# A decoder layer on one core: the statistics of the first norm in sums of four, their roots read from PSUM by ScalarE, and a set of constants made later

## The chip, the core and the metric

The kernel runs on one core of one Trainium2 chip. Its engines are called PE (TensorE's matmuls, with PEld for its weight loads), DVE (VectorE), ACT (ScalarE), POOL (GpSimd) and SP (SyncE, which here issues DMAs). Each has its own list of instructions and waits for others on semaphores. The metric is device time of one execution in microseconds (us), lower is better. Three runs of the kernel before gave a median of 2107.65 us (2106.93 to 2108.5). About 0.2% of it, 4.2 us, can be told from no change.

## The reference

All in float32, with x of 2 batches x 512 tokens x 1024. The change lies in the first lines: the layer norm and the first projection of the Mamba block.

```python
x = x + attn(_layernorm(x))          # Mamba-2 block and a gated MLP
x = x + xattn(_layernorm(x), ctx)    # quantised matmul with the context
x = x + ffn(_layernorm(x))           # three matmuls with binarised differences

def _layernorm(x, axis=-1, eps=1e-05):
    m = jnp.mean(x, axis=axis, keepdims=True)
    v = jnp.var(x, axis=axis, keepdims=True)
    return (x - m) / jnp.sqrt(v + eps)

# attn begins:
h = hidden * rsqrt(mean(hidden * hidden) + EPS) * ln1_w
zxbcdt = h @ w_in.T                                   # w_in: 2568 x 1024
z, xs, Bs, Cs, dt = split(zxbcdt, [1024, 1280, 1536, 2560])
xBC = silu(causal_conv4(concat(xs, Bs, Cs)) + conv_b) # 12 tiles of 128 columns
dt = softplus(dt + dt_bias)                           # 8 columns, one for each head
# ... chunked state space scan with dt, cumulative sums of dt * A, gate by silu(z), @ w_out
```

## The kernel before

The tokens lie in the free dimension, the 1024 features on 128 partitions x 8 blocks (k = 0 to 7). A batch is one half of 512 columns. For exact float32 products each operand is split in a rounded high part and the rest, and a product is three matmuls (hi x hi, lo x hi, hi x lo); ACT writes the high part (`weights_hi`, `act_hi`), DVE subtracts it for the low one (`weights_lo` L1737, `act_lo` L2095).

The **head** (to about 57 us) takes one batch after the other. DVE adds the blocks in pairs (`head_pair` L2084), PE sums the four pairs over the partitions by matmuls with a matrix of 1/1024 (`head_mean` L866), DVE takes the mean from each block (`head_centre` L2089), ACT makes `act_hi` (L1532) and the squares (L1520), DVE `act_lo`. PE multiplies each block, as it becomes ready, with the first two blocks of weights (`first_half` L882, six matmuls for a block and a batch). DVE adds the squares in pairs (L2101), PE sums them (`head_var` L873), DVE scales the sum (L2105), ACT takes logarithm and exponential of it (`head_root` L1525, L1526, behind a table load L1523), and DVE mends the root by a Newton step (`head_rsqrt` L2110 to L2112). The tables of constants (`constants` L1747 to L1771, 23 small instructions of DVE) stand between the two batches. The products of the normed input with the 8 columns for dt (L913, L915, 32 matmuls) follow when both batches are through.

The **conv stage** (57 to 176 us) has six pairs of weight blocks. A block is 48 matmuls (L849) on PE. DVE multiplies what comes out by the root (L2162), makes the low part of the weights two blocks on (L1737), and runs the four taps of the convolution (L2168, three of L2170); ACT applies silu and makes `weights_hi`. PE starts a block when its weights are ready (`raw_consumed`) and DVE has taken the product that was in the same bank (`conv_product_taken`). After the third pair DVE clears `minus_cs_wide` (L2221) and scales six blocks of the input (L2187). In the middle of the fifth pair DVE writes the cumulative sums into `minus_cs_wide` (L2231), which PE transposes (L936) before the sixth pair.

Every engine works through its list in the order that is written, so an instruction that waits holds up all that stands behind it on its engine.

## Time and profile before

| | |
|---|---|
| Median of three runs | 2107.65 us |
| Profiled execution, its own time | 2109.02 us |
| Its span, first to last instruction | 2106.9 us |
| PE busy | 2081.3 us (99%) |
| DVE busy | 1679.2 us (80%) |
| ACT busy | 1055.6 us (50%) |
| Mean granted TensorE clock | 0.998 |

### The profile page before, as it was taken

The numbers are of one execution on the slowest core, as the hardware profiler recorded it, in microseconds if no ns is written. First come the engines' busy times: TensorE is split into PE (matmuls) and PEld (weight loads), VectorE is DVE, ScalarE is ACT, GpSimd is POOL, SyncE is SP. The second block draws the span as 40 slices with busy tenths as digits, with TensorE's granted clock in tenths as the row PEclk, the third lists the DMA queues.
The fourth block names the chain that finished last, engine by engine and source line by source line (L and its number), as shares of the span: only waits on it lengthen the run. The fifth ranks groups of instructions, "written<-read, shape, count | busy, mean of one in ns | idle before, by whom it ended". The sixth has DMA issues, their size and how long they took to land.

```text
span 2106.9 us, 26518 instructions
## 1 busy us (share of the span) xinstructions
PE 2081.3 (99%) x9230; PEld 1670.4 (79%) x9234; DVE 1679.2 (80%) x2526; ACT 1055.6 (50%) x1748; POOL 186.1 (9%) x296
## 2 busy tenths in 40 slices
PE   8999999999999999999999999999999999999999
PEld 4777778788888888888888855888888888888887
DVE  8888686797777888888879898977677776698886
ACT  5333244457777777774444366533333333444442
POOL 0001101101111112110000002010000000100000
PEclk9999999999999999999999999999999999999999
DMA  3151116539889999897430045554444443846101
GB/s 137 38 206 54 51 61 196 149 112 324 289 298 332 326 348 351 294 343 263 141 140 1 1 180 116 170 195 147 171 146 175 161 150 123 321 176 208 52 21 60
DMA packets 136434, 370.07 MB, mean 176 GB/s; under 512 B 16688, under 2 KB 27568, under 8 KB 132656
## 3 DMA queue, kind: packets, MB, share of 16 engines
q1 hardware_dynamic: 110640, 287.12, 39.1%
q0 software_dynamic: 25088, 80.23, 11.1%
q8 instruction: 74, 1.21, 0.2%
q10 hardware_dynamic: 576, 1.05, 0.1%
q14 instruction: 56, 0.46, 0.1%
HBM read 288.12 MB, written 84.41 MB: 177 GB/s over the span
## 4 chain that ended last, share of the span: by engine, by line
PE 88%; DVE 9%; ACT 2%; issue 1%; DMA 0%; ACTq 0%; DVEq 0%
PE pair L1086 47%; PE pair L1134 24%; PE pair L856 7%; PE pair L1030 2%; DVE conv_out L2170 2%; PE pair L849 1%; PE pair L1096 1%; PE pair L1167 1%; DVE weights_lo L1737 1%; PE pair L968 1%; PE pair L989 1%; PE pair L1161 1%; PE pair L995 0%; DVE comb_lo L1905 0%; DVE hs L2089 0%
## 5 line engine op out<-in xcount | busy, mean ns | idle before, releaser
L1086 PE MATMUL pair<-comb_hi,ring_hi 128*128 128x512 f32 x1456 | 566.7, 389 | 0.0
L1086 PE MATMUL pair<-comb_hi,ring_lo 128*128 128x512 f32 x1456 | 566.5, 389 | 0.0
L1086 PE MATMUL pair<-comb_lo,ring_hi 128*128 128x512 f32 x1456 | 566.5, 389 | 0.0
L1134 PE MATMUL pair<-inner_ring_a,ring_hi 128*128 128x512 f32 x1080 | 332.8, 389 | 0.0
L1086 PEld LDWEIGHTS pair<-comb_hi,ring_hi 128*128 128x128 f32 x1456 | 273.3, 188 | 58.1 <-issue 1.4
L1086 PEld LDWEIGHTS pair<-comb_lo,ring_hi 128*128 128x128 f32 x1456 | 273.3, 188 | 56.8
L1086 PEld LDWEIGHTS pair<-comb_hi,ring_lo 128*128 128x128 f32 x1456 | 273.3, 188 | 56.6
L1134 PEld LDWEIGHTS pair<-inner_ring_a,ring_hi 128*128 128x128 f32 x1080 | 202.6, 188 | 42.1
L1134 PE MATMUL pair<-inner_ring_a,ring_lo 128*128 128x512 f32 x540 | 210.1, 389 | 0.0
L1360 ACT ACTIVATE ring_hi<-ring_sum 128x512 fp32r<-128x512 f32 x160 | 100.5, 631 | 147.4 <-DVE ring_sum L1818 145.4
L1833 DVE TENSOR_TENSOR ring_lo<-raw_a,ring_hi 128x512 fp32r<-128x512 f32 x146 | 99.7, 688 | 54.6 <-ACT ring_hi L1360 52.8
L1134 PE MATMUL pair<-inner_ring_b,ring_hi 128*128 128x512 f32 x432 | 133.5, 390 | 0.0
L1134 PEld LDWEIGHTS pair<-inner_ring_a,ring_lo 128*128 128x128 f32 x540 | 101.3, 188 | 21.1
L1833 DVE TENSOR_TENSOR ring_lo<-ring_sum,ring_hi 128x512 fp32r<-128x512 f32 x160 | 109.9, 687 | 10.0 <-ACT ring_hi L1360 7.8
L856 PE MATMUL pair<-act_hi,weights_hi 128*128 128x512 f32 x256 | 108.5, 424 | 1.7 <-DVE act_lo L2272 1.4
L1984 DVE TENSOR_TENSOR pair<-coeff_in 128x1024 f32<-128x1024 f32 x84 | 103.1, 1227 | 0.0
L856 PE MATMUL pair<-act_hi,weights_lo 128*128 128x512 f32 x256 | 100.0, 390 | 0.0
L856 PE MATMUL pair<-act_lo,weights_hi 128*128 128x512 f32 x256 | 99.8, 390 | 0.0
L1486 ACT ACTIVATE sign_out<-pair 128x1024 int8<-128x1024 f32 x84 | 85.3, 1016 | 24.3 <-DVE pair L1984 24.3
L1134 PEld LDWEIGHTS pair<-inner_ring_b,ring_hi 128*128 128x128 f32 x432 | 81.1, 188 | 17.3 <-issue 0.5
L1360 ACT ACTIVATE ring_hi<-raw_a 128x512 fp32r<-128x512 f32 x146 | 87.4, 624 | 10.6 <-DVE raw_a L1813 7.0
L1360 ACT ACTIVATE ring_hi<-comb_hi_f 128x512 fp32r<-128x512 f32 x72 | 45.4, 630 | 94.0 <-PE pair L1134 47.9
(395 smaller groups left out, 3616.1 us busy)
## 6 DMA issues: line engine op xcount, KB each, us to landing
coeff_in<-f_gu SPq DMA_DIRECT2D x56, 512.0 KB, 5.2
coeff_in<-b_gu SPq DMA_DIRECT2D x56, 512.0 KB, 7.0
weights_raw<-w_mamba SPq DMA_DIRECT2D x44, 512.0 KB, 3.5
raw_a<-w_gu SPq DMA_DIRECT2D x28, 512.0 KB, 6.2
raw_a<-w_gu SPq DMA_DIRECT2D x56, 256.0 KB, 6.0
u_spill<-gate_a POOLq DMA_DIRECT2D x56, 256.0 KB, 5.2
coeff_in<-f_dn SPq DMA_DIRECT2D x28, 512.0 KB, 4.5
coeff_in<-b_dn SPq DMA_DIRECT2D x28, 512.0 KB, 6.7
```

Of the source, the lines that this page charges most:

```text
L849: ins = pe.matmul(out[:, HALF[half]], w[:, wi, k * P:(k + 1) * P], a(half, k), start=k == 0 and n == 0, stop=k == KT - 1 and n == 2)
L856: ins = pe.matmul(out, w[:, wi, k * P:(k + 1) * P], a(b, k), start=k == 0 and n == 0, stop=k == KT - 1 and n == 2, skip_group_check=True)
L968: pe.matmul(ps[2][:, g * 512:(g + 1) * 512], bx_cur[:, 2 + g, :], xbc[:, 4 + g * HPG:4 + (g + 1) * HPG, b * SEQ + c * P:b * SEQ + (c + 1) ...
L989: ins = pe.matmul(ps[2][:, hd * P:(hd + 1) * P], x_dt[:, hd, :], att[:, hd, :], start=True, stop=c == 0)
L1030: ins = pe.matmul(out, wt[:, slot, col], a, start=j % 2 == 0 and kk == 0 and n == 0, stop=j % 2 == 1 and kk == KH - 1 and n == 2, skip_gro ...
L1086: ins = pe.matmul(out, wt[:, slot, col], a, start=t in (0, 1, 3) and kk == 0 and n == 0, stop=kk == KH - 1 and n == 2, skip_group_check=True)
L1134: ins = pe.matmul(out, wt[:, slot, col], a, start=t in (0, 1, 3) and k == 0 and n == 0, stop=k == SC_PAIRS - 1 and n == 2, skip_group_chec ...
L1360: act.activation(WRH[:, slot, :], src, ACT.Copy).then_inc(s_whi, 1)
L1486: act.activation(sign_out[:, c % 2, :], dif_ps[:, :], ACT.Sign).then_inc(s_sign, 1)
L1833: TT(WRL[:, slot, :], src, WRH[:, slot, :].bitcast(F32), ALU.subtract).then_inc(s_wlo, 1)
L1984: TT(dif_ps[:, :], dif[:, c % 2, 0, :], dif[:, c % 2, 1, :], ALU.subtract).then_inc(s_cd, 1)
L2170: ins = STT(tile[:, :, back:], src[:, :, :SEQ - back], conv_par[:, s, TAPS - 1 - back:TAPS - back], tile[:, :, back:], ALU.mult, ALU.add)
```

## The change

In the head, for the second batch the four pair sums are added to two by DVE (`head_four`) before PE sums them, and so are the squares of the first batch; the squares of the second batch stay four pair sums. The eight products for dt of the first batch stand on PE before the second batch's blocks (`dt_half`), those of the second behind its variance. The first batch's variance stands on PE behind block 4 of the second, and two of the four variance products of the second batch behind its block 6. ACT reads the variance sums from PSUM, with scale and bias in the instruction, for the logarithm and for a copy that DVE's Newton step uses; DVE's scaling goes. ACT's wait for the first root moves from behind block 4 to behind block 6, and one of two table loads goes. The constants, but for the two instructions on `w_dt`, move behind the third pair of the conv stage. The low part of the fourth weight block (`weights_lo(4, 1, 1)`) moves from ahead of the second root to behind the first product of the conv stage. Waits that count semaphores are renumbered to suit.

```diff
         for k in range(KT):
             first_half(k, 0)
-            if k >= KT // 2:
-                head_mean(1, k - KT // 2)
-        head_var(0)
+            if k == KT - 2:
+                head_mean(1, 0, 0, 7, False)
+        head_mean(1, 1, 2, 10, True)
+        pe.wait_ge(s_const, 3)
+        dt_half(0)
         for k in range(KT):
             first_half(k, 1)
-        head_var(1)
+            if k == 4:
+                head_var(0, 0, 4, 15, False)
+                head_var(0, 1, 8, 16, True)
+            if k == 6:
+                head_var(1, 0, 4, 17, False)
+                head_var(1, 1, 6, 18, False)
+        head_var(1, 2, 8, 19, False)
+        head_var(1, 3, 10, 20, True)
+        dt_half(1)
...
         def head_root(b):
-            act.preload_act_table_set("natural_log_exp_and_others")
-            act.wait_ge(s_ht, b + 1)
-            own.then(act.activation(scr_u(4)[:, HALF[b]], scr_u(6)[:, HALF[b]], ACT.Ln))
+            act.wait_ge(s_hvar, HEAD_VARS[b])
+            own.then(act.activation(scr_u(4)[:, HALF[b]], ps[3][:, HALF[b]], ACT.Ln, bias=EPS * EPS, scale=(1.0 + EPS) / DM))
             act.activation(root_in[:, HALF[b]], scr_u(4)[:, HALF[b]], ACT.Exp, scale=-0.5).then_inc(s_hroot, 1)
+            act.activation(scr_u(6)[:, HALF[b]], ps[3][:, HALF[b]], ACT.Identity, bias=EPS * EPS, scale=(1.0 + EPS) / DM).then_inc(s_ht, 1)
...
-                if b == 1 and k == 4:
+                if b == 1 and k == 2:
+                    act.preload_act_table_set("natural_log_exp_and_others")
+                if b == 1 and k == 6:
                     head_root(0)
...
+        def head_four(b, first, second, sums):
+            dve.wait_ge(s_hpair, sums)
+            TT(xbc[:, first, HALF[b]], xbc[:, first, HALF[b]], xbc[:, second, HALF[b]], ALU.add).then_inc(s_hpair, 1)
...
+            if k == 3:
+                dt_weights()
             if k >= KT // 2:
                 head_pair(1, k - KT // 2)
-        for j in range(KT // 2):
-            head_square_pair(0, j)
-        constants()
+            if k == KT // 2 + 1:
+                head_four(1, 0, 1, 6)
+        head_four(1, 2, 3, 9)
+        head_square_pair(0, 0)
+        head_square_pair(0, 1)
         head_centre(1, 0)
         head_centre(1, 1)
+        head_square_pair(0, 2)
         for k in range(KT):
             if k + 2 < KT:
                 head_centre(1, k + 2)
             head_lo(1, k)
-            if k == 1:
-                head_var(0)
-            if k >= 3 and k % 2 == 1:
-                head_square_pair(1, (k - 3) // 2)
-        head_square_pair(1, KT // 2 - 1)
+            if k == 0:
+                head_square_pair(0, 3)
+            elif k == 1:
+                head_four(0, 4, 6, 12)
+            elif k == 2:
+                head_four(0, 8, 10, 14)
+            elif k < 5:
+                head_square_pair(1, k - 3)
+            elif k > 5:
+                head_square_pair(1, k - 4)
         head_rsqrt(0)
         weights_lo(3, 0, 0)
-        weights_lo(4, 1, 1)
-        head_var(1)
         head_rsqrt(1)
...
             TT(conv_in, ps[s][:, :], root_in, ALU.mult).then_inc(s_taken, 1)
+            if n == 0 and s == 0 and lo is None:
+                weights_lo(4, 1, 1)
...
         conv_pair(2)
+        constants()
         dve.memset(cs_wide[:, :, :], 0.0)
         scale_hs(range(2, KT))
         conv_pair(3)
```

The order of ACT in the second batch of the head, the stretch that holds the first root. Before:

```order
L1532 ACTIVATE act_hi<-hs,params 128x512 [waits norm_centred]
L1520 ACTIVATE conv_out<-hs 128x512
L1523 ACT_TABLE_LOAD
L1525 ACTIVATE scratch_r<-scratch_r 128x512 [waits norm_var_ready]
L1526 ACTIVATE scratch_r<-scratch_r 128x512 [waits act_steps]
L1532 ACTIVATE act_hi<-hs,params 128x512 [waits norm_centred]
L1520 ACTIVATE conv_out<-hs 128x512
L1532 ACTIVATE act_hi<-hs,params 128x512 [waits norm_centred]
L1520 ACTIVATE conv_out<-hs 128x512
L1532 ACTIVATE act_hi<-hs,params 128x512 [waits norm_centred]
L1520 ACTIVATE conv_out<-hs 128x512 x3
```

And the same engine now, from `act_hi` of block 5 on (`pair` is PSUM, `conv_out` in the head holds the squares):

```order
L1543 ACTIVATE act_hi<-hs,params 128x512 [waits norm_centred]
L1531 ACTIVATE conv_out<-hs 128x512
L1543 ACTIVATE act_hi<-hs,params 128x512 [waits norm_centred]
L1531 ACTIVATE conv_out<-hs 128x512
L1535 ACTIVATE scratch_r<-pair 128x512 [waits norm_var_summed]
L1536 ACTIVATE scratch_r<-scratch_r 128x512 [waits act_steps]
L1537 ACTIVATE scratch_r<-pair 128x512
L1543 ACTIVATE act_hi<-hs,params 128x512 [waits norm_centred]
L1531 ACTIVATE conv_out<-hs 128x512 x3
```

The root has moved from between blocks 4 and 5 to between blocks 6 and 7; it waits on PE's sums themselves, and one `act_hi` and three squares stand behind it.

The order of DVE from the second root to the first taps of the conv stage. Before, from the first root's last step:

```order
L2112 SCALAR_TENSOR_TENSOR scratch_r<-scratch_r 128x512 [waits dve_steps]
L1737 TENSOR_TENSOR weights_lo<-weights_raw,weights_hi 128x1024 [waits weights_hi_ready,dve_steps]
L1737 TENSOR_TENSOR weights_lo<-weights_raw,weights_hi 128x1024 [waits weights_hi_ready]
L2105 TENSOR_SCALAR scratch_r<-pair 128x512 [waits norm_var_summed]
L2110 SCALAR_TENSOR_TENSOR scratch_r<-scratch_r 128x512 [waits norm_root_ready]
L2111 TENSOR_TENSOR scratch_r<-scratch_r 128x512 [waits dve_steps]
L2112 SCALAR_TENSOR_TENSOR scratch_r<-scratch_r 128x512 [waits dve_steps]
L2178 COPY conv_par<-params 128x10 [waits conv_summed,dve_steps]
L2162 TENSOR_TENSOR scratch_r<-pair,scratch_r 128x1024 [waits conv_summed,block_used,dve_steps]
L2168 TENSOR_SCALAR conv_out<-scratch_r,conv_par 128x1024 [waits conv_product_taken]
```

And now:

```order
L2127 SCALAR_TENSOR_TENSOR scratch_r<-scratch_r 128x512 [waits dve_steps]
L1750 TENSOR_TENSOR weights_lo<-weights_raw,weights_hi 128x1024 [waits weights_hi_ready,dve_steps]
L2124 SCALAR_TENSOR_TENSOR scratch_r<-scratch_r 128x512 [waits norm_root_ready]
L2126 TENSOR_TENSOR scratch_r<-scratch_r 128x512 [waits norm_var_ready,dve_steps]
L2127 SCALAR_TENSOR_TENSOR scratch_r<-scratch_r 128x512 [waits dve_steps]
L2203 COPY conv_par<-params 128x10 [waits conv_summed,dve_steps]
L2185 TENSOR_TENSOR scratch_r<-pair,scratch_r 128x1024 [waits conv_summed,block_used,dve_steps]
L1750 TENSOR_TENSOR weights_lo<-weights_raw,weights_hi 128x1024 [waits weights_hi_ready]
L2193 TENSOR_SCALAR conv_out<-scratch_r,conv_par 128x1024 [waits conv_product_taken]
```

One `weights_lo` has moved from ahead of the second root's wait to between the first product and its taps.

The order of DVE between the third and the fourth pair of the conv stage. Before:

```order
L2170 SCALAR_TENSOR_TENSOR conv_out<-scratch_r,conv_par,conv_out 128x2x509 [waits dve_steps]
L2221 MEMSET minus_cs_wide 128x576
L2187 TENSOR_TENSOR hs<-hs,scratch_r 128x1024 x6
L2178 COPY conv_par<-params 128x10 [waits conv_summed]
L2162 TENSOR_TENSOR scratch_r<-pair,scratch_r 128x1024 [waits conv_summed,block_used,dve_steps]
L1737 TENSOR_TENSOR weights_lo<-weights_raw,weights_hi 128x1024 [waits weights_hi_ready]
```

And now, the last four of the constants and what follows them:

```order
L1783 TENSOR_REDUCE row_scale<-tri_ident_mask 128x1 [waits dve_steps]
L1784 TENSOR_REDUCE row_scale<-tri_ident_mask 128x1 [waits dve_steps]
L1785 TENSOR_TENSOR row_scale<-row_scale 128x1 [waits dve_steps]
L2247 MEMSET minus_cs_wide 128x576 [waits dve_steps]
L2212 TENSOR_TENSOR hs<-hs,scratch_r 128x1024 x6
L2203 COPY conv_par<-params 128x10 [waits conv_summed]
L2185 TENSOR_TENSOR scratch_r<-pair,scratch_r 128x1024 [waits conv_summed,block_used,dve_steps]
L1750 TENSOR_TENSOR weights_lo<-weights_raw,weights_hi 128x1024 [waits weights_hi_ready]
```

The constants (21 rows in all) stand ahead of the clearing, the six scalings and the low weights of the ninth block.

## Rows read from the trace of the kernel before

**Rows 1.** Chain of waits, 110 to 160 us (start us, us, what).
```profile
125.28 1.13 DVE weights_lo L1737
...
150.39 0.40 DVE minus_cs_wide L2231 x3
...
150.83 2.71 PE pair L936 x16
```

**Rows 2.** Waits of PE, 60 to 200 us (total us, times, longest).
```profile
PE pair L936 <- DVE minus_cs_wide L2231: 2.3, 1, 2.3
...
PE pair L849 <- DVE weights_lo L1737: 0.8, 1, 0.8
```

**Rows 3.** Busy time by windows (stretch, us, engines with counts, PEclk, DMA).
```profile
126.40:130.00 3.60, 3.53 (x15) 2.92 (x16) 3.49 (x5) 0.00 (x0) 0.00 (x0) 1.00 1.04 400
148.50:150.80 2.30, 0.03 (x1) 0.00 (x0) 2.23 (x9) 0.74 (x1) 0.00 (x0) 1.00 0.22 75
150.80:155.40 4.60, 4.57 (x21) 4.15 (x22) 1.85 (x2) 2.66 (x3) 0.00 (x0) 0.63 0.45 162
```

**Rows 4.** Timeline of PE, head (start us, us, engine, line, what).
```profile
30.31 1.02 PE L866 MATMUL pair<-conv_out,ones_over_dm 128*128 128x512 f32 x2
31.16 3.60 PE L873 MATMUL pair<-conv_out,ones 128*128 128x512 f32 x8
...
44.12 0.39 PE L882 MATMUL pair<-act_hi,weights_hi 128*128 128x512 f32 x1
...
45.48 0.39 PE L882 MATMUL pair<-act_hi,weights_hi 128*128 128x512 f32 x1
...
49.88 0.79 PE L913 MATMUL pair<-act_hi,w_dt_hi_lo 128*16 128x512 f32 x1
...
57.68 0.62 PE L849 MATMUL pair<-act_hi,weights_hi 128*128 128x512 f32 x2
```

**Rows 5.** Timeline of DVE, 17 to 81 us.
```profile
17.75 0.75 DVE L2095 SCALAR_TENSOR_TENSOR act_lo<-hs,params,act_hi 128x512 fp32r<-128x512 f32 x1
18.42 0.68 DVE L2089 TENSOR_TENSOR hs<-hs,pair 128x512 f32<-128x512 f32 x1
...
28.34 0.22 DVE L1747 CAST ident_bf<-tri_ident_mask 128x128 bf16<-128x128 f32 x1
...
28.61 0.19 DVE L1749 CAST w_dt_hi_lo<-w_dt 128x64 fp32r<-128x64 f32 x1
...
29.11 0.16 DVE L1752 TENSOR_TENSOR minus_head_pick<-tri_ident_mask 128x8 f32<-128x8 f32 x1
...
31.79 0.16 DVE L1771 TENSOR_TENSOR row_scale<-row_scale 128x1 f32<-128x1 f32 x1
32.28 1.88 DVE L2089 TENSOR_TENSOR hs<-hs,pair 128x512 f32<-128x512 f32 x3 [0.33 <-DVE row_scale L1771]
...
52.75 0.69 DVE L2110 SCALAR_TENSOR_TENSOR scratch_r<-scratch_r 128x512 f32<-128x512 f32 x1 [1.36 <-ACT scratch_r L1526]
...
55.14 1.23 DVE L2162 TENSOR_TENSOR scratch_r<-pair,scratch_r 128x1024 f32<-128x1024 f32 x1
56.40 0.81 DVE L2168 TENSOR_SCALAR conv_out<-scratch_r,conv_par 128x1024 f32<-128x1024 f32 x1
...
78.14 1.23 DVE L2162 TENSOR_TENSOR scratch_r<-pair,scratch_r 128x1024 f32<-128x1024 f32 x1
...
80.42 0.81 DVE L2168 TENSOR_SCALAR conv_out<-scratch_r,conv_par 128x1024 f32<-128x1024 f32 x1
```

**Rows 6.** Timeline of ACT, second batch of the head.
```profile
39.87 0.63 ACT L1525 ACTIVATE scratch_r<-scratch_r 128x512 f32<-128x512 f32 x1
40.54 0.63 ACT L1526 ACTIVATE scratch_r<-scratch_r 128x512 f32<-128x512 f32 x1
41.07 0.71 ACT L1532 ACTIVATE act_hi<-hs,params 128x512 fp32r<-128x512 f32 x1
41.69 0.62 ACT L1520 ACTIVATE conv_out<-hs 128x512 f32<-128x512 f32 x1
```

More of the change, by code:

```diff
@@ L32 @@
 ORDER = (1, 0)
+HEAD_SUMS = 20
+HEAD_VARS = (2, 6)
 Y_AT = {5: (0, 1, 2), 6: (3, 4, 5), 7: (6, 7)}
@@ L861, in _, with head_mean, head_var, dt_half @@
         pe.sem_inc(s_stage, 1)
-        def head_mean(b, j):
-            pe.wait_ge(s_hpair, b * (KT // 2) + j + 1)
-            ins = pe.matmul(ps[2][:, HALF[b]], ones_mean[:, :], xbc[:, j, HALF[b]], start=j == 0, stop=j == KT // 2 - 1)
-            if j == KT // 2 - 1:
+        def head_mean(b, n, tile, sums, last):
+            pe.wait_ge(s_hpair, sums)
+            ins = pe.matmul(ps[2][:, HALF[b]], ones_mean[:, :], xbc[:, tile, HALF[b]], start=n == 0, stop=last)
+            if last:
                 ins.then_inc(s_hm, 1)
-        def head_var(b):
-            for j in range(KT // 2):
-                pe.wait_ge(s_hpair, KT + b * (KT // 2) + j + 1)
-                pe.matmul(ps[3][:, HALF[b]], ones[:, :], xbc[:, 4 + 2 * j, HALF[b]],
-                          start=j == 0, stop=j == KT // 2 - 1).then_inc(s_hvar, 1)
+        def head_var(b, n, tile, sums, last):
+            pe.wait_ge(s_hpair, sums)
+            pe.matmul(ps[3][:, HALF[b]], ones[:, :], xbc[:, tile, HALF[b]], start=n == 0, stop=last).then_inc(s_hvar, 1)
+        def dt_half(b):
+            for k in range(KT):
+                pe.matmul(ps[2][0:2 * HEADS, HALF[b]], wdt_hl[:, k, :, :], ah(b, k),
+                          start=k == 0, stop=False, skip_group_check=True)
+                ins = pe.matmul(ps[2][0:HEADS, HALF[b]], wdt_hl[:, k, 0, :], al(b, k),
+                                start=False, stop=k == KT - 1, skip_group_check=True)
+            if b == 1:
+                ins.then_inc(s_dtm, 1)
         def first_half(k, b):
@@ L906, in conv_pair @@
                 conv_block(i, s)
-        pe.wait_ge(s_const, 4)
-        for b, half in enumerate(HALF):
-            for k in range(KT):
-                pe.matmul(ps[2][0:2 * HEADS, half], wdt_hl[:, k, :, :], ah(b, k),
-                          start=k == 0, stop=False, skip_group_check=True)
-                ins = pe.matmul(ps[2][0:HEADS, half], wdt_hl[:, k, 0, :], al(b, k),
-                                start=False, stop=k == KT - 1, skip_group_check=True)
-        ins.then_inc(s_dtm, 1)
         conv_pair(1)
@@ L1198, in _ @@
         feed_forward(W_END[0] - 4, W_END[0] - 2)
-        ctx_var(bank(1), x_square_a, range(KH), 2 * KT, (), 0)
+        ctx_var(bank(1), x_square_a, range(KH), HEAD_SUMS, (), 0)
         feed_forward(W_END[0] - 2, W_END[0])
@@ L1218, in _ @@
         column_sums(1, bank(3))
-        ctx_var(bank(7), x_square, range(KH), 2 * KT + KH, (), 0)
+        ctx_var(bank(7), x_square, range(KH), HEAD_SUMS + KH, (), 0)
         pe.wait_ge(s_mc, 2)
@@ L1246, in _ @@
         pe.wait_ge(s_xt, 6)
-        ctx_var(bank(7), x_square, range(KH), 2 * KT + 2 * KH, (), 0)
+        ctx_var(bank(7), x_square, range(KH), HEAD_SUMS + 2 * KH, (), 0)
         pe.wait_ge(s_rlo, 2)
@@ L1265, in _ @@
         pe.wait_ge(s_ht, 4 + BATCH + 2)
-        ctx_var(bank(7), x_square, range(3), 2 * KT + 3 * KH, (6, 7), 5 * KT)
+        ctx_var(bank(7), x_square, range(3), HEAD_SUMS + 3 * KH, (6, 7), 5 * KT)
         second_mean(0, bank(6))
@@ L1744, in _, with dt_weights @@
         dve.sem_inc(s_yt, 1)
+        def dt_weights():
+            own.then(dve.tensor_copy(wdt_hl[:, :, 0, :], wdt[:, :, :]))
+            TT(wdt_hl[:, :, 1, :], wdt[:, :, :], wdt_hl[:, :, 0, :].bitcast(F32), ALU.subtract).then_inc(s_const, 1)
         def constants():
-            dve.wait_ge(s_par, 48)
             dve.tensor_copy(ident_bf[:, :], ident).then_inc(s_const, 1)
             dve.tensor_copy(mask_bf[:, :], mask).then_inc(s_const, 1)
-            own.then(dve.tensor_copy(wdt_hl[:, :, 0, :], wdt[:, :, :]))
-            own.then(TT(wdt_hl[:, :, 1, :], wdt[:, :, :], wdt_hl[:, :, 0, :].bitcast(F32), ALU.subtract))
             dve.memset(coef3[:, :], 0.0)
@@ L2124, in _ @@
                 head_centre(0, k + 3)
+            if k == 3:
+                dt_weights()
             if k >= KT // 2:
                 head_pair(1, k - KT // 2)
-        for j in range(KT // 2):
-            head_square_pair(0, j)
-        constants()
+            if k == KT // 2 + 1:
[3 more added lines that the diff above has]
+        head_square_pair(0, 1)
         head_centre(1, 0)
         head_centre(1, 1)
+        head_square_pair(0, 2)
         for k in range(KT):
```

8 lines of the change are left out of this document (3 added, 5 removed).

## Prediction

> **What bounds the kernel now.** I read the chain of waits first, then the waits of PE, then timelines of PE, DVE and ACT over the first 160 us, since all that is changed lies there. PE is busy nearly throughout, so it seems to be the bound. The chain says otherwise for the start: up to 150.8 us it runs over DVE, with the low weights of the ninth block and the writing of `minus_cs_wide`, and only from L936 on over PE [rows 1]. PE's waits agree: 0.8 us for those low weights and 2.3 us at L936 for DVE [rows 2]. So until L936 PE has 3.1 us to spare, and an edit there is worth what it does to DVE's arrival at `minus_cs_wide` (150.39). What follows is PE's own work and what PE releases, and it shifts with L936.
>
> One more thing hangs on that wait. In the wait PE is at the full clock in the records, and in 150.8 to 155.4 the mean granted clock is 0.63: most of it was at 1.2 GHz. Behind the 0.8 us wait it stays at 1.00 (2.4 GHz) [rows 3]. The low stretch took PE (1 - 0.63) x 4.6 = 1.7 us, on the chain.
>
> **The change, part by part.** I follow the changed lists in the durations of the rows: a DVE sum or centring steps by 0.60 (1.88 for three, the first ones overlapped), `act_lo` by 0.67 and is done after 0.75 [rows 5]; a float32 product with `ones` steps by 0.85 (30.31 to 31.16) and is done after 1.02, with handover 1.1; six matmuls of a block by 1.36 (44.12 to 45.48) [rows 4]; on ACT logarithm 0.67, exponential 0.53 (done 0.63), `act_hi` 0.62, square done after 0.62 [rows 6].
>
> *Start of the second batch.* Before, the fourth mean product starts at 30.31 with three such products in front of it among the blocks [rows 4]; now one stands in front of the last. Two less are 1.7 us. Against that DVE has the two instructions on `w_dt` (28.61 to 29.11, 0.5) and a sum of 0.6 to 0.7 ahead of the last `act_lo`, for which I allow PE a wait of 0.4. So the last product starts at 29.0, and the first centring at 30.1 to 30.2, where it was 32.28 behind the constants [rows 5]: 2.1 us won.
>
> *DVE's work there.* It gains four sums (two for the means, two for the squares) and the first batch's last two pair sums, and loses a scaling. Two centrings, a pair sum and a third centring (2.4) bring `act_lo` of block 0 to 32.6; each further block is centring, a sum and `act_lo`, 1.87. Block 4 starts at 32.6 + 4 x 1.87 = 40.1 and is done at 40.8. The eight dt products of the first batch take 16 of the 32 matmuls between 49.88 and 57.68 [rows 4], 3.9 us; from 29.9 to 33.7 they lie beside this and cost at most 0.3 at its start.
>
> *The new wait.* ACT now waits behind block 6 for the first variance, and PE makes it behind block 4: 40.8 + 1.36 = 42.2, two products, 0.85 + 1.1, so 44.2. ACT has stood there since about 41.4. Queued behind its wait are `act_hi` of block 7 and the squares of 5 to 7. Logarithm, exponential and the copy (0.67 + 0.53 + 0.53) end at 45.9, `act_hi` 0.62, square of block 5 done at 47.2. DVE stands too, as its next sum needs that square and `act_lo` of block 7 is behind the sum: 0.60 + 0.75, 48.6. PE, which had block 7 at 45.48 [rows 4], has it at 48.6. Then 1.36, two variance products (0.85 + 1.1) to 52.0, logarithm and exponential (0.67 + 0.63 and handover) to 53.4. There DVE's Newton step starts, 52.75 before [rows 5]. The 2.1 us are gone and 0.7 more.
>
> ACT reading PSUM with scale and bias is not in these rows; the nearest are a square at 0.62 and `act_hi`, which has a scale, at 0.71 [rows 6]. So it is between nothing and 0.1 more for each of four instructions; I take the logarithm's own 0.63, being the same function. The copy for the second root is hidden by the Newton step's first instruction (0.69). The table load that goes lay in a wait of ACT for DVE, so it gives nothing.
>
> *`weights_lo(4, 1, 1)`.* It stood in front of DVE's wait for the second root (1.36 idle [rows 5]), part of it free. Now it stands between the first product of the conv stage and its taps: with such an instruction there the step is 78.14 to 80.42, 2.28, without it 55.14 to 56.40, 1.26 [rows 5]. That is 1.0 more.
>
> *The constants.* What moves is 28.34 to 28.61 and 29.11 to 31.95, 3.1 us, and there were 0.33 us idle behind it [rows 5]: 3.1 to 3.45, I take 3.3. Behind the third pair DVE has no idle time to lay it in, and behind it are queued the clearing, six scalings, the next product and the low weights of block nine, for which PE already waited. POOL's store of the scaled input starts later by as much, and SP's loads, which wait for `raw_consumed`, move along; before, none of them held PE.
>
> DVE's arrival at `minus_cs_wide`: 0.7 + 1.0 + 3.3 = 5.0 us later. It hides what PE saves: four float32 products (3.4 us) fewer and the dt products earlier. PE would end the head about 2 us earlier (51.8 + 3.9 = 55.7 against 57.68), but the next block waits for the first product to be taken, 55.8 + 1.23 = 57.1.
>
> *The clock.* PE gets to block nine half a microsecond to one later than before and its weights come 5.0 later, so it waits 4 to 5 us there. That is longer than the wait at L936, behind which the clock fell, so I expect it to fall here, with up to 1.7 us lost in block nine. PE had 2.3 us to spare at L936, so this costs nothing in the end; it leaves 0.6 us of wait at L936, and behind a wait of 0.8 the clock did not fall [rows 2, 3]. The low stretch behind L936 then goes: 1.7 us back.
>
> Sum: + 5.0 - 1.7 = + 3.3 us. The profiled execution (2109.02, of it 2106.9 span) would be 2112.3; it lay 1.4 us above the median of the runs, 2107.65, which gives 2111.0.
>
> [...]
>
> **The rivals.**
> *Low clock twice (slower).* If the remaining wait at L936 is still followed by the low clock, nothing comes back, and the end is 5.0 us later: 2112.7. It decides if that wait stays near 2.3 us, as it does where the clock's fall lies mostly inside the long wait itself and costs block nine little. For it: the fall behind L936 came at once, within its 2.7 us [rows 1, 3]. Against it: block nine starts the work again right behind the wait, where a low stretch costs most.
> *PE is the bound after all (faster).* If the constants and the moved low weights find room on DVE, the four products less count: 2107.65 - 3.4 = 2104.2. Against it are both waits of PE for DVE.
> *ACT's wait does not bite.* If the first variance comes by the time ACT asks for it, about 3 us of the head come back; with 1.0 and 3.3 paid and the clock's 1.7 returned, DVE is 2.0 later and the end 0.3 later: 2108.0. Against it: the variance products stand behind block 4, whose `act_lo` DVE cannot give before 40.
>
> **How the numbers follow.** I give the forecast 0.66, the low clock twice 0.19, ACT's wait not biting 0.09, PE as the bound 0.06. The forecast's own range is 2109.6 to 2112.4: 0.35 either way for the constants, 0.4 for ACT's instructions, 0.5 for the head's handovers, and half a microsecond between runs. With the rivals, 8 in 10 lie in 2108.2 to 2113.2. The bound of 0.2% is 4.2 us: slower means over 2111.9, faster under 2103.4. Of the forecast a fifth lies above (0.13), of the first rival most (0.16): slower 0.29. Faster has the tail of PE as the bound, 0.04. The rest, 0.67, is the same within 0.2%.
>
> **What would show it.** Right: in the head ACT idle for about 3 us behind a square, waiting for L874, and DVE idle about 4 us in the middle of the second batch; the first product of the conv stage near 55.8; the constants as some 3 us of DVE ahead of the six scalings; PE waiting 4 to 5 us for the low weights of block nine with the low clock behind it, and less than 1.5 us at L936 with the full clock behind. Wrong: PE waiting at neither place, or DVE idle just ahead of the moved constants. A wait at L936 of over 2 us with the low clock behind it would be the first rival.

## The result and the profile after

The changed kernel takes 2114.44 us (median of 13 runs, 2111.3 to 2115.31), the kernel before 2107.65 (13 runs beside them, 2105.66 to 2111.2): the ratio is 1.0029, 95% interval 1.0022 to 1.0036, so 4.6 to 7.6 us slower; the medians lie 6.8 apart. The forecast was 2111.0, with a range of its own of 2109.6 to 2112.4 and one with the rivals to 2113.2, and it gave slower than 2111.9 a chance of 0.29: the direction was right, the size about half, and the time lies above both ranges. The profiled execution took 2115.17 us, its span is 2113.2.

The chain of waits of the changed kernel answers to [rows 1] (start us, us, what); the constants now stand in it, ahead of the scalings, and so do the low weights of block nine.

```profile
117.54 1.28 DVE conv_out L2195
118.82 0.14 DVE ident_bf L1763
...
121.71 0.16 DVE row_scale L1785
122.05 0.54 DVE minus_cs_wide L2247
122.59 6.75 DVE hs L2212 x6
129.46 1.23 DVE scratch_r L2185
130.68 1.13 DVE weights_lo L1750
...
155.78 0.40 DVE minus_cs_wide L2257 x3
156.22 1.97 PE pair L947 x16
```

`minus_cs_wide` is copied at 155.78, 5.39 us later than before, and L947 (L936 before) starts as much later. PE's waits from 60 to 200 us answer to [rows 2] (total us, times, longest):

```profile
PE pair L851 <- DVE weights_lo L1750: 3.1, 2, 1.9
PE pair L1000 <- DVE attention L2326: 0.8, 1, 0.8
PE pair L947 <- DVE minus_cs_wide L2257: 0.6, 1, 0.6
```

The wait for the low weights has grown from 0.8 to two waits of 3.1 together, and the wait at L947 has shrunk from 2.3 to 0.6. The windows answer to [rows 3] (stretch, us, busy of PE, PEld, DVE, ACT and POOL, PEclk, DMA):

```profile
81.00:90.00 9.00, 7.76 (x25) 6.14 (x26) 8.05 (x8) 2.00 (x2) 0.00 (x0) 0.62 0.18 58
130.00:132.00 2.00, 0.14 (x1) 0.14 (x2) 2.00 (x3) 0.00 (x0) 1.22 (x2) 1.00 0.37 147
132.00:140.00 8.00, 8.00 (x29) 6.37 (x29) 5.66 (x6) 3.29 (x3) 0.00 (x0) 0.79 1.01 369
155.00:157.20 2.20, 1.55 (x12) 1.13 (x11) 2.17 (x8) 1.73 (x2) 0.00 (x0) 1.00 0.32 102
157.20:162.00 4.80, 4.80 (x28) 4.09 (x26) 1.97 (x3) 1.67 (x2) 0.00 (x0) 1.00 0.35 134
```

Behind L947 the clock stays full, as forecast; PE is at 1.2 GHz for part of block nine (0.79), as forecast, and also at 82 us (0.62), which was not. The head, on PE, ACT and DVE, answers to [rows 4 to 6]:

```profile
29.87 1.02 PE L868 MATMUL pair<-conv_out,ones_over_dm 128*128 128x512 f32 x2
...
41.58 0.50 PE L891 MATMUL pair<-act_hi,weights_hi 128*128 128x512 f32 x1 [0.20 <-DVE act_lo L2109]
...
43.08 1.88 PE L874 MATMUL pair<-conv_out,ones 128*128 128x512 f32 x4
...
49.31 0.50 PE L891 MATMUL pair<-act_hi,weights_hi 128*128 128x512 f32 x1
...
50.81 1.88 PE L874 MATMUL pair<-conv_out,ones 128*128 128x512 f32 x4
```

```profile
44.99 0.60 ACT L1535 ACTIVATE scratch_r<-pair 128x512 f32<-128x512 f32 x1 [2.85 <-PE pair L874]
45.62 0.63 ACT L1536 ACTIVATE scratch_r<-scratch_r 128x512 f32<-128x512 f32 x1
46.16 0.58 ACT L1537 ACTIVATE scratch_r<-pair 128x512 f32<-128x512 f32 x1
```

```profile
30.93 1.28 DVE L2103 TENSOR_TENSOR hs<-hs,pair 128x512 f32<-128x512 f32 x2 [1.24 <-PE pair L868]
...
47.90 0.69 DVE L2119 TENSOR_TENSOR conv_out<-conv_out 128x512 f32<-128x512 f32 x1 [3.86 <-ACT conv_out L1531]
...
54.02 0.69 DVE L2124 SCALAR_TENSOR_TENSOR scratch_r<-scratch_r 128x512 f32<-128x512 f32 x1 [0.85 <-ACT scratch_r L1536]
...
56.41 1.22 DVE L2185 TENSOR_TENSOR scratch_r<-pair,scratch_r 128x1024 f32<-128x1024 f32 x1
57.55 1.21 DVE L1750 TENSOR_TENSOR weights_lo<-weights_raw,weights_hi 128x1024 fp32r<-128x1024 f32 x1
58.68 0.81 DVE L2193 TENSOR_SCALAR conv_out<-scratch_r,conv_par 128x1024 f32<-128x1024 f32 x1
```

ACT waits 2.85 us and DVE 3.86, as forecast (3 and 4); the first product of the conv stage is at 56.41, 1.27 later than before (0.7 forecast).

### The profile page after: what moved, and what is told of

It is laid out like the page before. It is cut to its first block, busy times and chain, and to the rows that moved or that the text cites. A ratio compares the mean times of both kernels' runs of the same rounds, so it can differ in the third digit from the quotient of the medians.

```text
span 2113.2 us, 26506 instructions
## 1 busy us (share of the span) xinstructions
PE 2084.5 (99%) x9222; PEld 1672.7 (79%) x9226; DVE 1680.1 (80%) x2528; ACT 1055.6 (50%) x1749; POOL 184.8 (9%) x296
## 3 DMA queue, kind: packets, MB, share of 16 engines
q8 instruction: 74, 1.21, 0.2%
## 4 chain that ended last, share of the span: by engine, by line
PE 89%; DVE 7%; ACT 2%; issue 1%; DMA 1%; SPq 0%; ACTq 0%; DVEq 0%
PE pair L1097 47%; PE pair L1145 24%; PE pair L858 7%; PE pair L1041 2%; DVE conv_out L2195 2%; PE pair L851 1%; PE pair L891 1%; PE pair L1107 1%; PE pair L1178 1%; PE pair L979 1%; PE pair L1000 1%; DVE weights_lo L1750 1%; DMA sign_in_cd<-sign_spill 1%; PE pair L1172 1%; PE pair L1006 0%
```

## The experiments

Of every profile the table gives the first product of the conv stage, the step from it to the copy of `minus_cs_wide`, the copy, PE's wait for it, the time from L936's successor to the writing of `b_token_major`, all in us, and under "runs" the median less that of the kernel before, run beside it (where only a profile was taken, the one run's time).

| kernel | first product | step | copy | wait | to b | runs |
|---|---|---|---|---|---|---|
| before | 55.14 | 95.25 | 150.39 | 2.3 | 34.96 | |
| e6 before again | 55.40 | 95.23 | 150.63 | 2.3 | 33.36 | -0.7 |
| e11 before, third | 56.24 | 95.25 | 151.49 | 2.3 | 33.37 | 0.0 |
| e12 before, fourth | 55.57 | 95.25 | 150.82 | 2.3 | 33.35 | +0.1 |
| changed | 56.41 | 99.37 | 155.78 | 0.6 | 33.36 | +6.8 |
| e1 changed again | 56.27 | 99.41 | 155.68 | 0.7 | 33.32 | +5.5 |
| e16 changed, third | 57.32 | 99.42 | 156.74 | 2.3 | 34.97 | +8.1 |
| e2 constants in a wait | 57.09 | 97.01 | 154.10 | 1.5 | 33.33 | +4.0 |
| e3 low weights back | 56.29 | 98.41 | 154.70 | none | 33.29 | +3.1 |
| e4 before, constants moved | 55.96 | 98.41 | 154.37 | 0.7 | 33.36 | +3.2 |
| e7 constants back | 59.09 | 96.25 | 155.34 | 2.3 | 33.36 | +3.9 |
| e8 root behind block 7 | 56.46 | 99.44 | 155.90 | 2.3 | 34.98 | +4.7 |
| e9 variance back | 53.06 | 99.42 | 152.48 | none | 33.30 | +1.5 |
| e10 dt late | 56.62 | 99.42 | 156.04 | under 0.2 | 33.35 | +5.6 |
| e5 back in parts | 52.51 | 95.31 | 147.82 | 2.3 | 33.34 | -4.3 |
| e13 before, filled | 55.16 | 95.21 | 150.37 | 2.3 | 33.37 | +0.8 |
| e14 changed, filled | 55.77 | 99.41 | 155.18 | 0.7 | 33.36 | +4.5 |
| e15 parts, filled | 52.75 | 95.30 | 148.05 | 2.3 | 33.34 | -3.5 |

**The two terms behind the head.** e1 is the changed kernel unaltered.

> The changed kernel as it is, for a second profile of it. The chain theory (DVE's arrival at minus_cs_wide sets the time, and what PE does behind the conv stage only shifts) expects L947 again 5.0 to 5.5 us later than before, the end of the conv stage 3.5 to 4 us later, and the rest of the kernel the same length as before to within 0.5 us; then the whole is about 4 us slower. The tail theory (the 2.5 us that the first profile shows between 1220 and 1330 us belong to the change) expects those 2.5 us there again, and 6 us in all. If they are chance, the 1220 to 1330 stretch is as long as before in this profile or differs by another amount.

2113.86 us against 2108.38, ratio 1.0027 (1.0015 to 1.0038), so 3.2 to 8.0 us slower, about 4 expected; the step to the copy repeats to 0.04 us. The low stretches that the first profile showed in the tail at 1235.9 and 1293.9 us are missing (e16 has the first of them), and the span is 2109.7: their 2.5 us come and go with the run. e2 puts the constants into DVE's wait for the second norm's root:

```
             TS(scr(3), ps[3][:, :], scale, bias, ALU.mult, ALU.add).then_inc(s_ht, 1)
+            if between is not None:
+                between()
             dve.wait_ge(s_hroot, BATCH + n)
...
-        rsqrt(1, lambda j: scr_u(j + 1), 1.0 / DM, EPS)
+        rsqrt(1, lambda j: scr_u(j + 1), 1.0 / DM, EPS, constants)
...
         conv_pair(2)
-        constants()
```

> The changed kernel with the constants moved into DVE's wait for the root of the second norm (2.33 us idle in the profile of the changed kernel at 71.8 us). The chain theory expects 3.3 us less behind the third pair and about 0.9 us more at the root, so minus_cs_wide about 2.3 us earlier than in the changed kernel, and a time 2 to 2.5 us below it. The clock theory (PE's new short waits and the low clock behind them make the loss, not DVE's work) expects PE's wait for the low weights of block nine gone with the low clock behind it, but the end of the conv stage no more than 0.5 us earlier, and the time with it.

2112.39, ratio 1.0017 (1.0008 to 1.0026). The step falls by 2.4, about the 2.33 us that DVE waited there (up to 74.15 in the changed kernel's timeline); the rest of the 3.3 sticks out. The first product lies 0.8 later than in e1, so the copy comes 1.6 sooner; the time is 1.5 under e1's, where 2 to 2.5 were expected, and the two intervals overlap. PE does not wait for the low weights of block nine any more. e3 undoes the other term:

```
+        weights_lo(4, 1, 1)
         head_rsqrt(1)
...
-            if n == 0 and s == 0 and lo is None:
-                weights_lo(4, 1, 1)
```

> The changed kernel with the low part of the fourth weight block made ahead of the second root again, as before. DVE waited 0.85 us for that root in the changed kernel, so the chain theory expects the first product of the conv stage 0.3 us later, its taps 0.85 us earlier, and everything up to minus_cs_wide 0.85 us earlier; the time 0.5 to 1 us below the changed kernel. If the move cost nothing, as a wait behind it would take it up, minus_cs_wide stays where it is to 0.2 us.

2111.45, ratio 1.0019 (1.001 to 1.0028): the step falls by 1.0, and so does the copy. The time is 2.4 under e1's, more than the 0.5 to 1 expected; the intervals overlap here too. e4 is the kernel before with the constants alone moved behind the third pair (the two instructions on `w_dt` stay where they were):

```
-        constants()
+        dt_weights()
         head_centre(1, 0)
...
         conv_pair(2)
+        constants()
```

> The kernel before with the constants alone moved behind the third pair of blocks (the two instructions on w_dt stay between the batches). The chain theory expects the second batch's first centring 0.8 us earlier (PE's last mean product then sets it), the constants to cost 3.3 us later, minus_cs_wide 2.5 us later than before, PE waiting about 4 us for the low weights of block nine, and the time 0.8 us (if the low clock behind L936 goes) to 2.5 us above before. If PE were the bound, the time would be 0.6 us below before.

2111.54, ratio 1.0014 (1.0005 to 1.0023). The step is 3.16 longer than before. The head gives back less than the 0.8 expected: the first product comes at 55.96, against 56.24 in e11, the profile of before with the same low stretch of the clock at 14 us, so 0.3 sooner. Between the batches of the kernel before, the constants lay mostly in time in which DVE would have waited for PE's last mean product (33.10 in e4, with 3.44 us of waiting for it); the change took them out of a nearly free place. e7 puts them back in the changed kernel:

```
         head_square_pair(0, 1)
+        constants()
         head_centre(1, 0)
...
         conv_pair(2)
-        constants()
```

> The changed kernel with the constants between the two batches again, where they stood before; all else as changed. The chain theory: VectorE reaches the second batch 3 us later, but PE's eight dt products of the first batch stand ahead of its blocks and cover 2 of it or more; behind the third pair 3.1 to 3.3 us come back. The first product of the conv stage at 57.4 to 59.5, the step from it to the copy of minus_cs_wide 96.1 to 96.3 us (99.3 in the changed kernel, 95.25 before), the time 0 to 2.2 us under the changed kernel's. If the cost of the constants lay not in their place but in the clock, the step would stay over 98.

2112.35, ratio 1.0018 (1.0009 to 1.0027). The step is 96.25, the 1.0 of the low weights over before, but the head is 2.8 later: between the batches of the changed kernel, where PE's means come sooner, the constants cost nearly what they cost behind the third pair. Only in a wait are they free.

**The head.** e8 lets ACT do `act_hi` of block 7 and the squares ahead of the first root:

```
-                if b == 1 and k == 6:
-                    head_root(0)
...
             head_square(b, KT - 1)
+        head_root(0)
         weights_hi(2, 0)
```

> The changed kernel with ScalarE's first root behind the act_hi of block 7 and the squares, instead of behind block 6: what was queued behind the wait (act_hi of block 7, three squares) goes first. My forecast held that this wait costs the head some 3 us. If so, PE has block 7 some 2 us sooner than 49.3 us, the first product of the conv stage moves from 56.3 to about 53.5 to 54.5, and the time falls by 2 to 3 us. The rival: PE is what the head hangs on, since the eight dt products (3.9 us) stand ahead of its blocks and each block follows the one before without a gap; then the variance comes when PE gives it, the first product moves by less than 0.6 us, and the time by as little.

2113.16, ratio 1.0022 (1.0011 to 1.0033). The root runs without a wait and the 3.86 us in which DVE stood ahead of the last `act_lo` are gone, yet PE has block 7 at 49.07 instead of 49.31 (timelines of e8: ACT, then PE, then DVE):

```profile
45.18 0.60 ACT L1535 ACTIVATE scratch_r<-pair 128x512 f32<-128x512 f32 x1
```

```profile
47.76 1.88 PE L874 MATMUL pair<-conv_out,ones 128*128 128x512 f32 x4
49.07 0.80 PE L891 MATMUL pair<-act_hi,weights_hi 128*128 128x512 f32 x1
```

```profile
56.46 1.23 DVE L2184 TENSOR_TENSOR scratch_r<-pair,scratch_r 128x1024 f32<-128x1024 f32 x1
```

Block 4 starts 0.19 later in e8 (41.77), so the longest waits of the head in the changed kernel cost block 7 some 0.4 us and the first product 0.1: in e8 PE works without a gap from block 4 on, and its order alone sets the end. e10 takes the dt products out of that order ahead of the blocks:

```
-        dt_half(0)
         for k in range(KT):
             first_half(k, 1)
...
+        dt_half(0)
         dt_half(1)
```

> The changed kernel with the first batch's eight dt products (16 matmuls, 3.7 us of PE) at the end of the head beside the second's. If they cost what the order on PE suggests, the first block of the second batch starts up to 3.7 us sooner and the first product of the conv stage too. If VectorE's 1.87 us per block paces PE up to block 4 (PE waits 0.2 us for act_lo at each of blocks 2, 3 and 4 in the changed kernel), they are hidden: the first product stays within 0.4 us of 56.3 and the time within 1 us of the changed kernel's.

2113.11, ratio 1.0027 (1.0017 to 1.0037): hidden, first product at 56.62. In their place PE waits for the first `act_lo` of the batch, and the clock falls behind that wait; block 4 starts at 41.80 (41.58 in the changed kernel).

```profile
34.35 0.52 PE L891 MATMUL pair<-act_hi,weights_hi 128*128 128x512 f32 x1 [3.24 <-DVE act_lo L2109]
```

e9 takes back the variance by fours with its order on DVE, ACT and PE, puts the dt products late as e10 does, and leaves the rest (of the edit, the lines of PE's variance):

```
+        for j in range(KT // 2):
+            head_var(0, j, 4 + 2 * j, 11 + j, j == KT // 2 - 1)
         for k in range(KT):
             first_half(k, 1)
-            if k == 4:
-                head_var(0, 0, 4, 15, False)
-                head_var(0, 1, 8, 16, True)
-            if k == 6:
-                head_var(1, 0, 4, 17, False)
-                head_var(1, 1, 6, 18, False)
-        head_var(1, 2, 8, 19, False)
-        head_var(1, 3, 10, 20, True)
+        for j in range(KT // 2):
+            head_var(1, j, 4 + 2 * j, 15 + j, j == KT // 2 - 1)
```

> The changed kernel with the variance sums and products as before (by pairs, behind all blocks of a batch), the first root behind block 4 and the dt products at the end of the head; the second batch's mean by fours, the constants behind the third pair and the late low weights of the fourth block stay as changed. If VectorE's arrival is a plain sum of terms, the first product of the conv stage comes at 52.5 us (56.3 in the changed kernel), the step from it to minus_cs_wide stays 99.4, the copy comes at 151.9 and the time is 1 to 1.5 us over that of the kernel before, 4 to 4.5 under the changed kernel's. If the terms overlap (VectorE gives back what it won, because PE paces it between 56 and 148 us), the copy stays over 153.5 and the time 3 us or more over before.

2108.98, ratio 1.0009 (1.0 to 1.0018). The first product comes at 53.06, 3.2 to 3.4 sooner than in the first two profiles of the changed kernel, and the step stays 99.42: the terms add. The wait (e8) and the dt products (e10) being without effect, each taken away by itself, what cost the head is the variance by fours. PE's timelines share the 3.35 us in two: block 4 starts at 41.58 instead of 40.21, 1.4 later, and from there to the products for dt behind the last variance product PE takes 10.55 us instead of 8.57, 2.0 more. The first part is DVE's pace: it gives a block every 1.86 us up to block 4, where in e9 it gives the first four every 1.26 with no sum between them (`act_lo` of the first blocks, DVE, changed kernel and e9):

```profile
33.33 0.75 DVE L2109 SCALAR_TENSOR_TENSOR act_lo<-hs,params,act_hi 128x512 fp32r<-128x512 f32 x1
...
35.19 0.74 DVE L2109 SCALAR_TENSOR_TENSOR act_lo<-hs,params,act_hi 128x512 fp32r<-128x512 f32 x1
```

```profile
33.32 0.74 DVE L2105 SCALAR_TENSOR_TENSOR act_lo<-hs,params,act_hi 128x512 fp32r<-128x512 f32 x1
...
34.58 0.75 DVE L2105 SCALAR_TENSOR_TENSOR act_lo<-hs,params,act_hi 128x512 fp32r<-128x512 f32 x1
```

e5 is e9 with the low weights ahead of the second root and the constants split over two of DVE's waits, the second norm's root and the softplus exponential:

> Kept of the change: the second batch's mean from two sums of four, ScalarE reading the variance from PSUM, no constants between the batches. Back as before: the variance products by pairs behind all blocks of a batch, with the first root asked for behind block 4 of the second batch; the dt products at the end of the head; the low weights of the fourth block ahead of the second root. New: the constants lie in two of VectorE's waits, most of them while the second norm's root is made, the last few while the softplus exponential is made. The chain theory (everything before L936 is worth what it does to VectorE's arrival at minus_cs_wide): no instruction of VectorE is added ahead of the first product of the conv stage, the constants (3.1 us) leave its path, two float32 products leave PE's; the first product of the conv stage at 52.5 to 54 us (55.14 before), the copy of minus_cs_wide 1 to 2.6 us sooner than 150.39, and the time 1 to 3.4 us under that of the kernel before. PE then waits less or not at all at L936's successor. The rival (PE is the bound of the head whatever VectorE does, and the excess lies in low-clock stretches of the first 90 us): the time within 1 us of the kernel before.

2104.21 us against 2108.5, ratio 0.9982 (0.9973 to 0.9991): faster than both kernels, 3.8 us under before by the ratio. The step is that of before, 95.31, with all constants hidden, and the head is 3 us shorter. PE's wait at L936's successor is 2.3 as before, where less or none was expected, so DVE still sets the end there.

**The clock.** Three more profiles of before and one of the changed kernel:

> The kernel before, for a second profile. It tells whether the excess of the measured difference (5.5 to 6.8 us) over the 3.7 us seen at the end of the conv stage lies in the clock. If the extra low-clock stretches of the changed kernel (6.8 us instead of 3.4 at 14 us, one at 82 us, one at block nine) belong to its waits, the profile of before shows one of 3.4 us at 14 to 16 us, none at 82 and 133, one behind L936, again. If they come by chance of the run, this profile shows some of them as well, and minus_cs_wide then lies later than 150.39.

> The kernel before, a third profile, for the clock behind L936: PE waits 2.3 us there in both profiles so far, with 3.4 us at the low clock behind it in the one and none in the other. If the low stretch is a matter of chance, it is there in some of the profiles; L936 to the writing of b_token_major then takes 35.0 us with it and 33.4 without.

> The kernel before, a fourth profile, for the same question: 35.0 us from L936 to b_token_major with a low stretch behind the wait, 33.4 without one.

> The changed kernel, a third profile. In the first two the low clock of the head lasts 6.8 us; in before 3.4 in three profiles of four. If it is chance, this one may show 3.4 and the first product of the conv stage at 55.5 instead of 56.3; if it hangs on the change, 6.8 again. In the tail the first profile had low stretches at 1236 and 1294 us and the second none; L1207's successor to the second block there takes 59.2 or 57.5 us accordingly.

PE waits 2.3 us at L936 in all four of before, and in three no low clock follows; their runs took 2107.8, 2107.52 and 2107.56 us, against 2109.02 of the one with it. The windows behind it in e6 and e11, against 0.63 in [rows 3], and in e16, where the changed kernel has the wait of 2.3 and the low clock:

```profile
150.80:155.40 4.60, 4.33 (x27) 3.88 (x28) 1.69 (x5) 2.91 (x3) 0.00 (x0) 1.00 0.51 183
```

```profile
151.90:156.50 4.60, 4.57 (x28) 4.07 (x29) 1.11 (x1) 2.52 (x3) 0.00 (x0) 1.00 0.49 174
```

```profile
PE pair L947 <- DVE minus_cs_wide L2257: 2.3, 1, 2.3
```

```profile
157.20:161.80 4.60, 4.60 (x22) 4.12 (x23) 2.52 (x3) 2.61 (x3) 0.00 (x0) 0.64 0.45 167
```

Over all profiles here with a wait of 2.3 at that place the low clock follows in 3 of 10. At block nine the longer wait is not the surer one. In the first two profiles of the changed kernel and in e14 PE waits 1.9 to 2.0 us there, the clock falls behind it, and 0.6 to 0.7 are left at L947 with the full clock behind: the forecast's picture. In e16 and e8 PE waits 3.4 us at block nine, the clock stays at 1.00 (126 to 148 us), 2.3 are left at L947 and the low clock follows there: the sign that the forecast gave for its first rival. PE's waits for the low weights in e16:

```profile
PE pair L851 <- DVE weights_lo L1750: 4.6, 2, 3.4
```

In the head the low clock follows PE's wait of 3.8 us at 11 to 15 us in each of the fifteen profiles so far, but longer in the changed kernel (10 to 22 us of e6, then of the changed kernel):

```profile
10.00:22.00 12.00, 8.05 (x25) 5.03 (x24) 10.57 (x16) 9.53 (x15) 0.00 (x0) 0.86 0.82 310
```

```profile
10.00:22.00 12.00, 8.23 (x22) 5.55 (x21) 10.15 (x17) 9.16 (x14) 0.00 (x0) 0.72 0.83 315
```

It is 0.72 in all three of the changed kernel, and of before in e11 alone, whose first product is 0.67 to 1.1 us later than in the other three. e13, e14 and e15 fill that wait with four products whose result is not used, in before, in the changed kernel and in e5:

```
+        for _ in range(4):
+            pe.matmul(ps[3][:, HALF[0]], ones[:, :], xbc[:, 3, HALF[0]], start=True, stop=True)
```

> The kernel before with four float32 products more on PE, results unused, in its wait of 3.8 us for the first act_lo of the head (11 to 15 us); nothing else differs. The low clock at 14 to 17 us follows that wait: with the wait filled it should not come, whether it is 3.4 or 6.8 us long without. The first product of the conv stage then lies about 0.8 us ahead of 55.4 (a stretch longer by 3.4 us put it 0.85 later in one profile of before), at 54.3 to 54.8, minus_cs_wide at 149.5 to 150.1, and the time falls by 0.6 to 1.2 us. If the first blocks hang on VectorE rather than on PE, nothing changes.

> The changed kernel with the same four products in the same wait. If part of the measured difference is that the low clock of the head lasts 6.8 us in the changed kernel and mostly 3.4 in the one before, the two kernels with that wait filled stand closer: the changed one 4.0 to 4.6 us behind the other (the sum of 0.1 in the head, 1.0 for the low weights, 3.2 for the constants), its own gain being 1.2 to 2 us. If that stretch has nothing to do with the difference, both gain the same and 5.5 to 6.8 us stay between them.

> The version that undoes the change in parts (variance by pairs, low weights ahead of the second root, constants in VectorE's waits, the mean by fours kept), with the wait filled too. If the terms add, it gains what the kernel before gains by it, 0.6 to 1.2 us, and lies near 2103.4. If the stretch is hidden here, because VectorE has two sums more between the batches, it stays at 2104.2.

The low stretch is gone in all three (window of e14):

```profile
10.00:22.00 12.00, 11.20 (x38) 6.41 (x37) 10.62 (x17) 9.46 (x14) 0.00 (x0) 1.00 0.82 311
```

Before gains nothing by it (2108.45 against 2107.62, ratio 1.0002, 0.9993 to 1.0011; my 0.6 to 1.2 were wrong), e5 nothing (2104.14, ratio 0.9983, 0.9974 to 0.9992), but the changed kernel falls to 2112.12, ratio 1.002 (1.0011 to 1.0029): 4.5 us behind before, where it was 5.5 and 6.8. The intervals of these ratios overlap, so 1.0 to 2.3 us is no more than a likely size; in the profiles the first product comes 0.5 to 1.55 us sooner than in the unfilled changed kernel. Why the two differ in this is seen at the second batch's first centring. In e13 it stands behind the constants, as in before (32.28 in [rows 5]), and the filling does not move it; in the changed kernel it follows PE's last mean product (30.93 above) and comes sooner by as much as the first product does (e13, then e14):

```profile
32.31 1.88 DVE L2091 TENSOR_TENSOR hs<-hs,pair 128x512 f32<-128x512 f32 x3 [0.32 <-DVE row_scale L1773]
```

```profile
30.29 1.28 DVE L2105 TENSOR_TENSOR hs<-hs,pair 128x512 f32<-128x512 f32 x2 [1.06 <-PE pair L868]
```

Between the filled kernels 3.7 us stay. The copies of e13 and e14 lie 4.81 apart, the first products 0.61:

```profile
55.16 1.22 DVE L2164 TENSOR_TENSOR scratch_r<-pair,scratch_r 128x1024 f32<-128x1024 f32 x1
...
150.37 0.39 DVE L2233 COPY minus_cs_wide<-minus_cs_all 128x64 f32<-128x64 f32 x3
```

```profile
55.77 1.22 DVE L2187 TENSOR_TENSOR scratch_r<-pair,scratch_r 128x1024 f32<-128x1024 f32 x1
...
155.18 0.39 DVE L2259 COPY minus_cs_wide<-minus_cs_all 128x64 f32<-128x64 f32 x3
```

## Why the prediction was wrong

*What bounds the kernel: right.* In the table the runs follow the copy of `minus_cs_wide`, whatever moved it: 3.0 us sooner than the mean of before's four profiles (150.83) with e5's -4.3, 1.65 later with e9's +1.5, 4.85 later with e1's +5.5. PE waits there for 0.6 to 2.3 us in all but e3, e9 and e10. Behind the copy every profile takes 1953 to 1957.5 us to its end, whichever kernel it is: before 1953.9 to 1956.5, the changed kernel 1954.0 to 1957.4.

*DVE's arrival, + 5.0: right.* With the clock of the head equal (e13, e14) it is + 4.8: 0.61 in the head (0.7 forecast), and 4.20 in the step: 1.0 for the low weights (e3) and 3.2 for the constants (e4; 3.3 forecast).

*The head: the size right, by luck, the mechanism wrong in part.* DVE's pace of a block up to block 4 was in the forecast (1.87, measured 1.86). Behind that it let ACT's new wait hold up block 7 through DVE. The waits came in the forecast sizes, but e8 removes them and gains nothing at the first product: PE's own order takes as long. The cause is the variance by fours with its order (e9): its sums slow DVE's blocks, and two of its products stand in front of block 5 and two in front of block 7, in a row on PE.

*ACT reading PSUM with scale and bias: right,* 0.60 us for the logarithm beside 0.63 from SBUF ([rows 6]), and 0.58 for the copy. The Trainium skill (Perfetto Trace Analysis, section "Optimizing Scalar/DVE Operations") gives ScalarE a smaller fixed cost per instruction on PSUM than on SBUF; the rows agree, with 0.03 us between the two logarithms.

*PE at block nine: right in kind.* The wait was 4 to 5 by the forecast and is 1.9, because PE had already lost time to the wait of 1.24 us and the low clock at 82 us; in e9 and e10, without those, it is 4.0, and in e16 and e8, whose low clock at 82 us is the shorter, 3.4.

*The clock, - 1.7: this step failed.* I took the low stretch behind L936 for a property of its wait of 2.3 us. It is there in one profile of before out of four, and I had that one. It cost 1.6 us there (34.96 against 33.36 in the table), but the median of before's runs, 2107.65, is the time of the three profiled runs without it: there was next to nothing to save. The forecast saw that its profile lay 1.4 us above the median and carried the 1.7 over to the median all the same. The low stretch can also come in the changed kernel (e16, e8). Without this term the sum is + 5.0, 2112.7, inside the measured 4.6 to 7.6. That is also the first rival's price; its picture, a wait of over 2 us that stays at L947 with the low clock behind it, is there in one profile of the changed kernel of three. The Trainium skill (TensorE: Matmul & The Clock Gate, section "HAM oscillation — how this bites in real kernels") tells of a kernel in which each wait of about 3 to 5 us is followed by the low clock. The trace agrees for the wait of 3.8 us in the head (15 of 15) and not for the 3.4 us at block nine in e16 and e8; waits of 2.3 us, as at L936, are not in that section.

*What the forecast left out: the low clock at 14 us.* It lies ahead of all that the change moves, so I took it as equal. It is the longer one in all three profiles of the changed kernel and in one of four of before, and e14 gains by its going, 0.5 to 1.55 us at the first product, where e13 does not: before, the constants between the batches covered it unless it was long (e11), and the change took that cover away. In the unfilled profiles the copy lies 5.2 us later on average (156.07 against 150.83), 0.4 more than the 4.8 of DVE's own instructions, and the rest of the span is 1.2 us longer (1956.2 against 1955.0): 6.4 together, where the runs have 5.5 and 6.8.

*Open.* Why that stretch is longer is not shown: e4, which moves the constants alone, has it long, e5 short, and three profiles of three against one of four can be chance. What the 1.2 us behind the copy are is not shown either. The filled kernels stand 3.7 us apart in the runs and 4.8 in their copies; a low stretch behind L936's successor in some runs of e13 would do that, but the one profile has none. And the tail's low stretches (none to two, 2.5 us in the first profile) may differ between the kernels by more than chance; three and four profiles don't tell.

## What to carry to other kernels

A clock stretch that one profile shows behind a wait is one draw: take two or three profiles before a term of a sum rests on its going, since here a gain of 1.7 us hung on a stretch that is there one time in four. A long wait in the new order is not yet a cost: ask what its end would let start, and whether that engine is free then (3.9 us of DVE's idleness here cost the next stage 0.2 or less). Small constants cost their full time on the engine that paces, wherever they stand, except in one of its waits: split over two waits 3.2 us went to nothing, and where they first stood, ahead of a wait for PE, they cost about 0.3 (e4 against e11). Before moving such work, ask whether its old place was free.

## What the hardware showed

The clock fell behind shorter waits than at L936, and once behind none. At 82 us the changed kernel has sixteen products of 16 x 16 (1.95 us) and a wait of 1.24 ahead of the fall, and the products behind them take 1.21 for two instead of 0.62:

```profile
79.71 1.95 PE L933 MATMUL pair<-tri_ident_mask,scratch_r 16*128 16x16 f32 x16
82.90 1.21 PE L851 MATMUL pair<-act_hi,weights_hi 128*128 128x512 f32 x2 [1.24 <-DVE weights_lo L1750]
```

In all four profiles of before the same sixteen, with no wait behind them, leave the clock full (window of 60 to 100 us of one):

```profile
60.00:100.00 40.00, 40.00 (x185) 33.16 (x184) 32.61 (x41) 16.48 (x17) 0.00 (x0) 1.00 0.08 27
```

In e4 they have no wait behind them either, and the clock falls all the same, so the wait alone does not decide it (the pairs of products behind them step by 0.85 us, in before by 0.46):

```profile
80.39 1.95 PE L922 MATMUL pair<-tri_ident_mask,scratch_r 16*128 16x16 f32 x16
...
82.90 1.05 PE L849 MATMUL pair<-act_lo,weights_hi 128*128 128x512 f32 x2
83.75 1.05 PE L849 MATMUL pair<-act_hi,weights_lo 128*128 128x512 f32 x2
```

Such stretches cost nothing where DVE paces PE: e9's at block nine (6.8 us at 1.2 GHz from 127.4) leaves the step at 99.42. Of one program the runs spread over 2.7 to 6 us, and profiles of one program differ by which of these stretches they have.
